# A graph network in one kernel: the sort's second operand goes to PSUM by ScalarE, and two pairs of transfers become one transfer each

## The reference

```
x += segment_sum((h*W0)[src], dst)                         # layer 0
h1 = relu(mean(h[src]) @ W1_l.T + b1 + h @ W1_r.T)
x += mean(h1[src]) @ W2_l.T + b2 + h1 @ W2_r.T             # layer 1
eh = edge_attr @ W_fcr.T ; m = segment_max(eh, dst)
ex = exp(eh - m[dst]) ; alpha = ex / segment_sum(ex)[dst]
x += relu(segment_sum(alpha*(z[src] + eh)) + z @ loop_W)   # layer 2, z = h @ W_fc.T
x += segment_sum(h[dst] @ W3.T + b3, src) / deg            # layer 3: grouped by src
```

## Time and profile before

| | us |
|---|---|
| median of 3 runs | 12968.6 (12952.4 to 12992.1) |
| profiled execution, its own time | 13008.7 |
| its span, first to last instruction | 13006.3 |
| POOL busy | 7991.4 (61% of the span), of which gathers 7985.1 in 8320 |
| DVE busy | 3850.4 (30%) |
| PE busy | 3824.5 (29%) |
| ACT busy | 587.2 (5%) |

### The profile page before, as it was taken

How to read it: one execution, slowest core, us unless ns; L and a number is a source line. 1 busy time by engine, 2 the same in 40 slices (tenths; PEclk the granted TensorE clock), 3 DMA queues, 4 the chain that set the end, 5 groups by cost and what they waited for, 6 DMA issues and landing times.

```text
span 13006.3 us, 84556 instructions
## 1 busy us (share of the span) xinstructions
PE 3824.5 (29%) x18630; PEld 2915.4 (22%) x18631; DVE 3850.4 (30%) x4140; ACT 587.2 (5%) x826; POOL 7991.4 (61%) x8346
## 2 busy tenths in 40 slices
PE   2322232233333333212211123444444431111222
PEld 1111111122222222111111113333333321111111
DVE  3233232333333333343334421222222221111111
ACT  0000000011111111100000000000000000000000
POOL 5666666655555555577666756555555556666666
PEclk6555555566566666555555556666676665555555
DMA  3333333343334443212233212222222221111111
GB/s 113 89 96 101 90 100 96 83 118 118 118 118 120 130 120 116 80 35 49 55 55 60 49 33 59 62 63 60 62 65 61 61 49 35 35 37 37 35 36 35
DMA packets 700586, 953.61 MB, mean 73 GB/s; under 512 B 276913, under 2 KB 491953, under 8 KB 697533
## 3 DMA queue, kind: packets, MB, share of 16 engines
q0 software_dynamic: 266240, 385.62, 14.7%
q10 hardware_dynamic: 196544, 441.95, 11.1%
q1 hardware_dynamic: 237507, 123.00, 3.2%
HBM read 742.96 MB, written 206.15 MB: 73 GB/s over the span
## 4 chain that ended last, share of the span: by engine, by line
another core or an unknown queue 40%; issue 21%; DVE 8%; PE 7%; POOL 3%; DMA 3%; DVEq 2%; ACTq 2%; ACT 2%; SPq 1%; POOLq 0%
POOL flat L294 3%; DMA flat<-gate_d 3%; PE pair L1026 2%; DVE flat L632 1%; DVE flat L469 1%; DVE flat L633 1%; PE pair L1183 1%; PE flip L1092 1%; ACT flat L920 1%; PE flip L1093 1%; DVEq L469 1%; DVEq L221 1%; ACTq L866 1%; ACTq L856 0%
## 5 line engine op out<-in xcount | busy, mean ns | idle before, releaser
L294 POOL DMA_INDIRECT flat<-table,stage x8320 | 7985.1, 960 | 4992.2 <-issue 2439.9
L1026 PE MATMUL pair<-flat 128*128 x9760 | 1439.0, 316 | 4344.3 <-issue 2406.8
L1026 PEld LDWEIGHTS pair<-flat 128*128 x9760 | 1108.2, 124 | 4751.1 <-issue 4694.3
L469 DVE TENSOR_TENSOR flat<-fixed,dcol 128x1024 f32 x915 | 1080.2, 1218 | 1939.8 <-remote 1134.2
L1183 PE MATMUL pair<-flat 128*128 x4880 | 1127.8, 397 | 1610.6 <-DVE flat L740 1406.3
L1183 PEld LDWEIGHTS pair<-flat 128*128 128x128 f32 x4880 | 1032.1, 239 | 1700.6 <-issue 1698.1
L511 DVE TENSOR_REDUCE batch<-pair 128x65 f32<-128x195 f32 (+1 forms) x392 | 139.2, 355 | 2694.8 <-remote 2041.3
L1092 PE MATMUL flip<-ident,flat 128*128 128x128 f32 x840 | 355.9, 425 | 1395.7 <-ACT flat L920 827.8
L1040 PE MATMUL wide<-flat,wbd 128*128 128x512 f32 x840 | 570.4, 824 | 444.0 <-issue 310.0
L740 DVE TENSOR_TENSOR flat<-fixed,dcol 128x512 f32<-128x512 f32 x610 | 404.2, 686 | 837.6 <-remote 577.9
L469 DVE TENSOR_TENSOR flat<-fixed,flat 128x1024 f32 x305 | 360.4, 1219 | 766.3 <-remote 565.7
(11 more groups left out here) (142 smaller groups left out, 1961.9 us busy)
## 6 DMA issues: line engine op xcount, KB each, us to landing
flat<-table,stage POOLq DMA_INDIRECT x8320
flat<-in_ea ACTq DMA_DIRECT2D x140, 768.0 KB
ex_d<-flat ACTq DMA_DIRECT2D x140, 768.0 KB
flat<-ex_d SPq DMA_DIRECT2D x208, 512.0 KB
flat<-gate_d ACTq DMA_DIRECT2D x280, 192.0 KB
pm_d<-flat ACTq DMA_DIRECT2D x70, 768.0 KB
flat<-pm_d ACTq DMA_DIRECT2D x70, 768.0 KB
sort_d<-flat ACTq DMA_DIRECT2D x14, 1024.0 KB
```

The lines of the kernel that those rows point to most:

```text
L294: pool.indirect_dma_start(out=to_row, out_offset=None, in_=tables[p], in_offset=bass.IndirectOffsetOnAxis(ap=stage[:, st, c:c + 1].bitcast ...
L469: V.tensor_tensor(ohb[:, ds(v % OHB, 1), :, :].rearrange("p o k e -> p (o k) e"), base, col[:, ds(g * CH, CH)].unsqueeze(2).to_broadcast([ ...
L1026: mm = M(bank[a % 2][:, 0:width], flat[:, ds(at_one[k], P * 2)].bitcast(bf16), flat[:, ds(at_row[k], TW * 2)].bitcast(bf16)[:, 0:width], s ...
```

## The change

Three edits. The gates of both lines are loaded by one transfer, whose source reads row 0 of `gate_d` 64 times and then row 1 64 times, into all 128 partitions of `gate`. The exponents of both lines are stored by one transfer. The counts in the waits on `f_ld`, `b_ld` and `b_st` follow. In the sort, ACT copies the upper half of the pairs of each round into `copied`, the first 1024 columns of `wide` in PSUM, when the round before is done (`k_step`), and DVE waits for it (`k_half`) and reads its second operand there. Where the keys come from a reload, ACT waits for it first (`k_load`), as DVE does.

```diff
+        copied = wide[:, 0:KC // 2]
+        def lower(x, m, d):
+            return x.rearrange("p (u v w) -> p u v w", v=2, w=1 << d)[:, :, 0, :]
+        def upper(x, m, d):
+            return x.rearrange("p (u v w) -> p u v w", v=2, w=1 << d)[:, :, 1, :]
+        def partner(half, m, d):
+            return half[:, :, ::-1] if m <= LK and d == m - 1 else half
...
+            rounds_done = [0]
             def pairs(n, m, d):
                 x, y = keys[n % 2], keys[1 - n % 2]
-                if m <= LK and d == m - 1:
-                    xv, yv = [a.rearrange("p (u e) -> p u e", e=2 << d) for a in (x, y)]
-                    lo, up = slice(0, 1 << d), slice((2 << d) - 1, (1 << d) - 1, -1)
-                    ends = [(a[:, :, lo], a[:, :, up]) for a in (xv, yv)]
-                else:
-                    xv, yv = [a.rearrange("p (u v w) -> p u v w", v=2, w=1 << d) for a in (x, y)]
-                    ends = [(a[:, :, 0, :], a[:, :, 1, :]) for a in (xv, yv)]
-                (x0, x1), (y0, y1) = ends
+                x0, x1 = lower(x, m, d), partner(copied.rearrange("p (u w) -> p u w", w=1 << d), m, d)
+                rounds_done[0] += 1
+                dve.wait_ge(k_half, rounds_done[0])
                 dve.wait_ge(k_step, ksteps[0])
-                kstep(V.tensor_tensor(y0, x0, x1, ALU.min))
-                kstep(V.tensor_tensor(y1, x0, x1, ALU.max))
+                kstep(V.tensor_tensor(lower(y, m, d), x0, x1, ALU.min))
+                kstep(V.tensor_tensor(partner(upper(y, m, d), m, d), x0, x1, ALU.max))
...
             def load_gate(sm, h, e0):
-                act.dma_start(gate[h][0:F, :], gate_d[0, e0:e0 + SB].partition_broadcast(F)).then_inc(sm, 16)
-                act.dma_start(gate[h][F:P, :], gate_d[1, e0:e0 + SB].partition_broadcast(F)).then_inc(sm, 16)
+                act.dma_start(gate[h], gate_d[:, e0:e0 + SB].unsqueeze(1).to_broadcast([2, F, SB])).then_inc(sm, 16)
...
                     act.wait_ge(s1["flip_free"], u0 + NB + 2)
-                    for a in range(2):
-                        act.dma_start(ex_d[a, b * SB:(b + 1) * SB, :].rearrange("(p k) c -> p (k c)", k=BL),
-                                      exo[h][:, a, :, :].rearrange("p m c -> p (m c)")).then_inc(b_st[h], 16)
+                    act.dma_start(ex_d[:, b * SB:(b + 1) * SB, :].rearrange("a (p k) c -> p a (k c)", k=BL),
+                                  exo[h].rearrange("p a m c -> p a (m c)")).then_inc(b_st[h], 16)
                     if st + 2 < STEPS:
                         load_b(st + 2)
...
                 j = t // SEG
+                if t % SEG == SEG - 1 and j < len(bursts):
+                    if bursts[j][0] != "inner":
+                        act.wait_ge(k_load, 16 * (saves.index(j - 1) + 1))
+                    for r, (rm, d) in enumerate(bursts[j][1]):
+                        done, n = marks["round", j, r]
+                        act.wait_ge(k_step, done)
+                        S.activation(copied.rearrange("p (u w) -> p u w", w=1 << d), upper(keys[n % 2], rm, d),
+                                     ACT.Copy).then_inc(k_half, 1)
```

More of the change, by code:

```diff
@@ L201, in gnn_kernel @@
         b_st = [sem(f"b_st{h}") for h in range(2)]
-        k_in, k_step, k_saved, k_load, k_tp, k_cp, k_idx = [
-            sem(n) for n in "k_in k_step k_saved k_load k_tp k_cp k_idx".split()]
+        k_in, k_step, k_half, k_saved, k_load, k_tp, k_cp, k_idx = [
+            sem(n) for n in "k_in k_step k_half k_saved k_load k_tp k_cp k_idx".split()]
         s_out = sem("s_out")
@@ L334, in _ @@
                     for h in range(2):
-                        sp.wait_ge(b_st[h], 32 * (STEPS // 2))
+                        sp.wait_ge(b_st[h], 16 * (STEPS // 2))
                     sp.dma_start(src_k, src_keys).then_inc(k_in, 16)
@@ L536, in _ @@
                         st, h = i * (2 * NS) + n, n % 2
-                        dve.wait_ge(f_ld[h], i * (48 * NS) + 48 * (n // 2 + 1))
+                        dve.wait_ge(f_ld[h], i * (32 * NS) + 32 * (n // 2 + 1))
                         dve.wait_ge(f_st[h], i * (16 * NS) + 16 * (n // 2))
@@ L572, in _ @@
                         st, h = i * (2 * NS) + n, n % 2
-                        dve.wait_ge(b_ld[h], i * (64 * NS) + 64 * (n // 2 + 1))
+                        dve.wait_ge(b_ld[h], i * (48 * NS) + 48 * (n // 2 + 1))
                         dve.wait_ge(b_carry, st)
@@ L652, in burst @@
                     n += 1
-                for m, d in rounds:
+                for r, (m, d) in enumerate(rounds):
+                    marks["round", j, r] = (ksteps[0], n)
                     pairs(n, m, d)
@@ L900, in maxima @@
             def maxima(st):
-                act.wait_ge(b_ld[st % 2], 64 * (st // 2 + 1))
+                act.wait_ge(b_ld[st % 2], 48 * (st // 2 + 1))
                 act.wait_ge(b_xe, st)
@@ L916, in _ @@
                         maxima(st + 1)
-                    act.wait_ge(b_st[h], 32 * (st // 2))
+                    act.wait_ge(b_st[h], 16 * (st // 2))
                     for j in range(NB):
@@ L1062, in _ @@
                         n = hb * NS + AT.index(a7)
-                        pe.wait_ge(f_ld[n % 2], i * (48 * NS) + 48 * (n // 2 + 1))
+                        pe.wait_ge(f_ld[n % 2], i * (32 * NS) + 32 * (n // 2 + 1))
                         settle(pe)
@@ L1097, in _ @@
                         st, h = i * (2 * NS) + n, n % 2
-                        pe.wait_ge(b_ld[h], i * (64 * NS) + 64 * (n // 2 + 1))
+                        pe.wait_ge(b_ld[h], i * (48 * NS) + 48 * (n // 2 + 1))
                         settle(pe)
```

## The result

The changed kernel takes 13077.1 us (median of 7 runs, 13022.8 to 13119.5) against 12968.6 (7 runs, 12944.5 to 13005.2) for the kernel before: ratio 1.0077, 95% interval 1.0051 to 1.0103, 108 us slower at the medians. Forecast were 13350, which is 381 slower. The direction and the range held, the size didn't: the loss is 0.28 of what I had.

A forecast was written before the change was run, and what follows sets the result against it. In pass 2 the consumers, held by ACT's wait for the gates, were taken to pace POOL. 13008.7 + 330 (gates, pass 2) + 10 (pass 1) + 40 (sort) = 13389, less 40 for profile over median: 13350 us, range 13000 to 13650.

The forecast's parts named there:

- The gates on two engines: Merged gate load: outermost dimension 2 confines it to two engines instead of sixteen, so gates land 8.1 us later.
- Net +7.0 us per block where the landing releases the chain. With the 42 tight blocks that is 295 us: Pass 2: 8.1 us later landing, less 1.1 of issue, charged to blocks whose first copy starts as L904 ends.
- 47 blocks at 8.1 us of landing less 1.1 of issue: Pass 2's gate term, +330 us: a count taken between 42 tight blocks and all 53 that the gates end.
- Rival C: Two engines, but PE's own stalls pace every block and hide the late gates: only pass 3's +40, 13009 us; chance 0.05.
- A: The forecast itself, 13350 us, with late gates lengthening pass 2; time from 13084 to 13570; chance 0.78.
- Pass 1, +10: Pass 1: gate loads issued a block ahead and covered by gathers, so late landing costs +10 us (0 to 100).
- The exponents' store, the issue only: Merged exponents' store: all 16 engines stay in use, bytes equal; only issue time is saved, counted in the gate term.
- The sort, +40: Pass 3: a quarter of 246 us longer rounds and of 95 us POOL relief reaches the end, +62 - 24.
- pass 3 at 2475 us: Sign in the profile after: pass 3 would last 2475 us, with POOL busy 1582.
- 0.33 and 0.13 from Exp's hand-overs: Sort round: hand-over DVE to ACT 0.33 us and back 0.13, parts of a 3.84 us round.
- let a quarter of both through: Pass 3: share of +246 us longer rounds and -95 us POOL relief taken to reach the time: +62 - 24.

The follow-up runs named there:

- the runs with 4 and 16: Kernel before with the gates in one transfer from a table repeating each line, outermost dimension 4 or 16: ratios 1.0011 and 0.9955 on a chip of about 12970 us.
- gates_one: Kernel before with only the gate loads made one transfer: 10714.2 us (0.9998) on the quick chip; repeated on the slow chip, 1.0042.
- pe_padded_again: Kernel before with 16 more idle semaphore instructions on PE ahead of each visit's matmuls in pass 5: 13158.9 us (1.0144) on the slow chip.
- sort_psum: Kernel before with only the sort's second operand copied to PSUM: 10624.8 us (0.9915) on the quick chip; repeated on the slow chip, 1.0042.
- sort_copy_unread: Kernel before with the sort's copies and waits as in the change, but DVE reading both operands from SBUF: 1.0073 on the slow chip.

## Why the prediction was off by the size

**The gates on two engines: right.** 2 of 16, shown by the packets, by the landing (9.0 to 16.3 us, forecast 9 to about 17) and by the runs with 4 and 16.

**"Net +7.0 us per block where the landing releases the chain. With the 42 tight blocks that is 295 us": wrong, this is the step.** The term was 330, 47 blocks at 8.1 us of landing less 1.1 of issue (381 - 52); it measured 54, and by the table above 113 for the landing less 58 for the issue. So it is the landing that was priced at more than three times its worth. I called a block tight when its first copy starts right behind L904, and took it that a copy that starts late ends late. The last copy is what issues the store and the next loads, and it waits for a signal from PE, `flip_full`. A block of pass 2 in the kernel before, ACT in order of time:

```profile
3862.74 1.45 ACT L904 ACTIVATE wide<-flat 128x1536 f32<-128x1536 f32 x1 [6.92 <-DMA flat<-gate_d]
3864.13 1.06 ACT L920 ACTIVATE flat<-flip 128x512 f32<-128x512 f32 x2
...
3871.74 0.60 ACT L920 ACTIVATE flat<-flip 128x512 f32<-128x512 f32 x1 [4.29 <-remote]
3875.30 0.60 ACT L920 ACTIVATE flat<-flip 128x512 f32<-128x512 f32 x1 [2.96 <-remote]
3875.92 0.81 ACTq L926 DMA_DIRECT2D ex_d<-flat  x2
...
3889.80 1.45 ACT L904 ACTIVATE wide<-flat 128x1536 f32<-128x1536 f32 x1 [7.42 <-DMA flat<-gate_d]
```

and the same block in the changed kernel:

```profile
3848.51 1.45 ACT L915 ACTIVATE wide<-flat 128x1536 f32<-128x1536 f32 x1 [14.36 <-issue]
3849.90 1.07 ACT L931 ACTIVATE flat<-flip 128x512 f32<-128x512 f32 x2
...
3853.77 1.33 ACT L931 ACTIVATE flat<-flip 128x512 f32<-128x512 f32 x2 [0.55 <-PE flip L1111]
3855.13 0.37 ACTq L936 DMA_DIRECT2D ex_d<-flat  x1
...
3874.30 1.45 ACT L915 ACTIVATE wide<-flat 128x1536 f32<-128x1536 f32 x1 [12.80 <-issue]
```

Both start right behind the maxima. In the first the last two copies start after 4.29 and 2.96 us of idle time, in the second after 0.55 and nothing, and from maxima to maxima it is 27.1 us against 25.8: the next gates land 16.1 us behind the end of their issue instead of 9.0, and the block is not longer. PE beside it, first before, then after:

```profile
3864.85 0.46 PE L1092 MATMUL flip<-ident,flat 128*128 128x128 f32 x1 [4.79 <-issue]
...
3868.28 0.42 PE L1093 MATMUL flip<-ident,flat 128*128 128x128 f32 x1
...
3875.89 2.57 PE L1026 MATMUL pair<-flat 128*128 x16 [3.31 <-issue]
```

```profile
3850.62 0.46 PE L1110 MATMUL flip<-ident,flat 128*128 128x128 f32 x1 [12.23 <-issue]
...
3854.04 0.42 PE L1111 MATMUL flip<-ident,flat 128*128 128x128 f32 x1
...
3857.44 2.14 PE L1044 MATMUL pair<-flat 128*128 x24
```

PE stood idle for 12.23 us instead of 4.79 while it waited for ACT, and then ran without the pause of 3.31 us.

What the copies wait for can be told more closely. The middle lines are the last transposes of the block. In the kernel before the profile has them done at 3868.70 (ends on PE are modelled), but the trace records the last two `flip_full` signals only at 3871.72 and 3875.27, and the copies start 0.02 and 0.03 us behind them; in the changed kernel the last copy starts 0.04 us behind the last transpose. Over the blocks of the third and fourth tile place ACT stands idle for 9.6 us between the six copies before and 5.3 after the change; 8.3 and 3.9 of that come after the recorded end of the transposes that the copy reads. In gates_one on the quick chip it is 1.6 us, and nothing of it comes after. So on the slow chip what comes late is PE's signal, or a transpose whose true end the record doesn't show; which of the two is open.

Over all blocks of these two tile places the landing is +7.0 us, the issue -1.8 (forecast -1.1), the six copies -4.4, and the period from maxima to maxima +0.7 and +0.8. In the second and fifth place the period grew by 7.5 and 2.9 us, and the first, whose next loads are not waited for, gave 7.3 back: 4.6 us for five blocks, 64 for the 14 batches, which is the pass's 63. The rows for this were at hand before: 1183 us idle before 420 copies of 0.59, which is 17 us per block of six, say that something else sets their pace, and I had looked only at the first of them. Rival C named that cover, at 0.05; the truth lies between it and A, nearer to C.

That the pauses around PE shrink when PE is kept waiting, and grow when it gets more instructions, fits a PE that on this chip is supplied with instructions too slowly and catches up while it waits. pe_padded_again speaks for it; that it is the supply, nothing here shows.

**Pass 1, +10:** not told apart; pass 1 is 2368 to 2384 us in the three profiles of the slow chip with the merged gates, and 2372 to 2386 in the six with the gates as before (2385 in the kernel before).

**The exponents' store, the issue only:** right; it is worth 0 (-16 to +35 us by the interval).

**The sort, +40:** measured 54 (34 to 77), right in sign and size, partly by luck. The sign that I had named, pass 3 at 2475 us, did not come: it is 2423 in the changed kernel's profile, 11 us shorter than before, and 2451 and 2452 in the two others with the plain copies, against 2401 to 2433 in the seven slow-chip profiles with the old sort. On average that is 27 us of the 54; where the rest arises no profile shows. A round takes 3.45 us, not 3.84: from DVE's end to ACT's start 0.04 us and back 0.03, where I had taken 0.33 and 0.13 from Exp's hand-overs. The longer bursts are +180 us of DVE and cost 95; the relief is 93 us of POOL and gives 41. I had let a quarter of both through; by the ratios it was about half of each, so the errors in the two shares and in the length of a round made up for each other in part.

**Profile and time.** The two profiled spans differ by 34 us only, as the profile before lay 40 over its median and the one after 34 under; I read the passes in them, and the sizes from the timed ratios.

## What to carry to other kernels

A wait that ends last is on the path only if what it releases also ends later: follow the whole group behind it to the instruction that issues the next load, and see what each of them waits for, before a lateness is multiplied by the number of waits. Give a broadcast load an outermost dimension that all engines can share, if need be by storing the small table several times (here eight, for -58 us on the slow chip). And where an engine gets its operand through another, cut the work into two independent halves, so that the copy of one runs under the other.

## What the runs showed of the hardware that was not expected

- One chip runs the kernel before in 10717 us, three others in 12970 to 12990. On the slower ones the traces have 1338 to 2176 register and semaphore instructions of PE at 0.6 to 0.8 us, and in the kernel before POOL waits up to 28.4 us for PE; on the quicker one there are at most 5 of the first, and no wait of POOL for PE is over 0.3 us. Gathers take 0.94 us on both. The mean granted clock hardly differs (0.59 to 0.60, and 0.61 to 0.62 on the quick chip). Why is open.
- So the sign of an edit can depend on the chip: sort_psum is 0.9915 on one and 1.0042 on the other.
- DVE's min and max of 512 columns take 0.68 us each but start every 0.60, and a PSUM operand costs nothing (1.22 us at 1024 columns either way).
- With the pauses of sort_copy_unread more gathers are slow (158) than with rounds back to back (92). In part its bursts are longer, 572 us in all against 409, and hold 307 gathers instead of 240; but the slow share in them also grows, from 35% to 49%, which is not explained. With the operand in PSUM none of the 401 gathers in the bursts is slow.
